# A pass of GpSimd before each scatter of the last two batch pairs, in place of waits on the shared expert, and two shared up products moved into the drain

## The reference, cut to what matters

```python
logits = x @ gate_weight.T                       # 4096 tokens, 64 experts
gidx = top_k(group_max(softmax(logits)), 3)      # 3 of 8 groups
topk_w, topk_i = top_k(masked_scores, 6)         # 6 experts for each token
pos = cumulative count of a token's expert, over all tokens in order
slot = flat * C + minimum(pos, C - 1)            # C = 96 rows for each expert
buf = zeros(E * C, H).at[slot].set(x[tok])
out = silu(buf @ Wg) * (buf @ Wu) @ Wd           # for each of 64 experts
y = sum over 6 of out[slot] * topk_w
shared = silu(x @ Sg.T) * (x @ Su.T) @ Sd.T      # for all tokens
result = x + layernorm(y + shared)
```

## Time and profile before

| what | value |
|---|---|
| median of three runs | 1271.32 us (1269.12 to 1275.74) |
| the profiled execution | 1273.42 us, of which its span is 1271.6 us |
| mean granted TensorE clock | 0.98 |
| PE busy | 1172.3 us (92%) |
| DVE busy | 943.0 us (74%) |
| ACT busy | 870.4 us (68%) |
| POOL busy | 658.9 us (52%), of which the 192 scatters to BUF take 201.3 us |

### The profile page before, as it was taken

How to read it: one execution, slowest core, us unless ns; L and a number is a source line. 1 busy time by engine, 2 the same in 40 slices (tenths; PEclk the granted TensorE clock), 3 DMA queues, 4 the chain that set the end, 5 groups by cost and what they waited for, 6 DMA issues and landing times.

```text
span 1271.6 us, 25022 instructions
## 1 busy us (share of the span) xinstructions
PE 1172.3 (92%) x7360; PEld 830.8 (65%) x7360; DVE 943.0 (74%) x2773; ACT 870.4 (68%) x2327; POOL 658.9 (52%) x742
## 2 busy tenths in 40 slices
PE   4899999999999999999999999999879798999984
PEld 1466766766676676676667667667635476878863
DVE  3897688789789889979988997988856245444536
ACT  3998779878877887887888788788624332333424
POOL 4564334336654655654565565566562624444556
PEclk9999999999999999999999999999988899999988
DMA  8686677867976765565566456456427389899676
GB/s 271 156 218 143 113 131 152 169 149 173 192 179 135 121 120 103 107 123 102 100 105 110 93 105 133 77 97 109 87 58 224 107 229 226 228 242 234 138 192 227
DMA packets 402184, 190.02 MB, mean 149 GB/s; under 512 B 319312, under 2 KB 386358, under 8 KB 402048
## 3 DMA queue, kind: packets, MB, share of 16 engines
q1 hardware_dynamic: 375968, 166.38, 58.3%
q0 software_dynamic: 16416, 11.70, 5.2%
q10 hardware_dynamic: 9664, 10.30, 2.8%
HBM read 75.32 MB, written 64.69 MB: 110 GB/s over the span
## 4 chain that ended last, share of the span: by engine, by line
PE 71%; DVE 10%; issue 6%; ACT 6%; DMA 6%; another core or an unknown queue 1%; SPq 1%; POOL 0%; ACTq 0%; DVEq 0%; POOLq 0%
PE bank L1151 15%; PE bank L1180 14%; PE bank L1195 11%; PE bank L1166 8%; PE bank L1212 8%; DMA Y<-W,wix 4%; PE bank L1336 3%; PE bank L1319 3%; PE bank L1244 3%; PE bank L1323 2%; PE bank L1278 1%; ACT P L1432 1%; DMA X<-in_x 1%; DVE nm L1627 1%; ACT unused L617 1%
## 5 line engine op out<-in xcount | busy, mean ns | idle before, releaser
L1432 ACT ACTIVATE P<-bank,nm 128x256 f32<-128x256 f32 x512 | 237.5, 470 | 106.4 <-DVE nm L1627 97.0
L1151 PE MATMUL bank<-RB,W 128*128 128x512 f16 x1076 | 276.7, 382 | 5.3 <-DVE W L820 3.9
L1180 PE MATMUL bank<-RB 128*128 128x256 f32 x1024 | 244.1, 381 | 10.1 <-issue 6.8
L1081 POOL TENSOR_SCALAR P<-P,rr 128x256 f32<-128x256 f32 x256 | 120.4, 478 | 251.9 <-DVE rr L1609 244.6
L831 POOL DMA_INDIRECT BUF<-RT,ix x192 | 201.3, 1048 | 78.7 <-issue 37.2
L1180 PEld LDWEIGHTS bank<-RB 128*128 128x128 f32 x1024 | 185.2, 191 | 34.6 <-ACT RB L1403 6.6
L1151 PEld LDWEIGHTS bank<-RB,W 128*128 128x128 f16 x1076 | 105.5, 99 | 124.4 <-issue 10.5
L1627 DVE TENSOR_REDUCE nm<-bank 128x2 f32<-128x512 f32 x256 | 174.0, 681 | 11.1 <-PE bank L1180 8.7
L1212 PE MATMUL bank<-W,O 128*128 128x256 f16 x1060 | 157.9, 274 | 6.8 <-issue 6.8
L1102 POOL DMA_INDIRECT Y<-W,wix x64 | 90.8, 1419 | 111.5 <-ACT W L1515 43.8
L1086 POOL TENSOR_TENSOR PH<-P,PH 128x512 f16<-128x512 f32 x86 | 101.3, 1178 | 87.9 <-ACT PH L1448 86.7
(11 more groups left out here) (251 smaller groups left out, 2032.5 us busy)
## 6 DMA issues: line engine op xcount, KB each, us to landing
RB<-in_ewT SPq DMA_DIRECT2D x24, 352.0 KB
BUF<-zrow SPq DMA_DIRECT2D x24, 321.0 KB, 3.3
W<-BUF ACTq DMA_DIRECT2D x58, 120.4 KB
HT<-in_ewT SPq DMA_DIRECT2D x18, 352.0 KB
HT<-in_wc SPq DMA_DIRECT2D x24, 256.0 KB, 4.4
HT<-in_ws SPq DMA_DIRECT2D x24, 256.0 KB, 5.1
Y<-zrow SPq DMA_DIRECT2D x20, 256.0 KB
X<-in_x SPq DMA_DIRECT2D x8, 512.0 KB, 4.5
```

The lines of the kernel that those rows point to most:

```text
L1081: r = eng.tensor_scalar(p, p, rr[:, w % 4, t:t + 1], SP_, ALU.mult, ALU.mult)
L1151: r = eng.matmul(bk_[:, :], W[:, m, a, c * 2048 + h * 128:c * 2048 + (h + 1) * 128], XT[:, bp % 2, b, c, :], start=(k == 0), stop=(k == n ...
L1180: r = eng.matmul(bS[u % 2][:, t * 256:(t + 1) * 256], QK[:, i % 2, 0, q * 256 + t * 128:q * 256 + (t + 1) * 128], QK[:, i % 2, 1, q * 256: ...
L1432: r = eng.activation(P[:, u % 2, t * 256:(t + 1) * 256], bS[u % 2][:, t * 256:(t + 1) * 256], ACT.Exp, bias=nm0[:, u % 4, t:t + 1], accum_ ...
```

## The change

Three things change. The table `REST` goes. Instead each of the 48 scatters of batch pairs 6 and 7 (`bp >= PAUSE_FROM`) is led by one GpSimd `tensor_scalar` over 128 x 256 zeros (`still`, float32) into scratch (`pause`, float16), which counts up a new semaphore, and the scatter waits until it has. And the up products U1 and U2 move from the head of the tail into the drain slots 257 and 259 of PE, with h0 and s1 in slot 257 of ACT and a1 in slot 258 of DVE.

```diff
-TAIL_ORDER = {'pe': 'U1 U2 U3 U4 D0 U5 ...
- 'dve': 'c6 l0 c7 a1 c10 a2 ...
- 'act': 'h0 s1 s2 h1 s3 ...
+TAIL_ORDER = {'pe': 'U3 U4 D0 U5 ...
+ 'dve': 'c6 l0 c7 c10 a2 ...
+ 'act': 's2 h1 s3 ...
-    ("pe", 257): [("PV", 4), ("WO", 7), ("WO", 6), ("bg", 0)],
+    ("pe", 257): [("PV", 4), ("WO", 7), ("WO", 6), ("U", 1), ("bg", 0)],
-    ("pe", 259): [("PV", 4), ("WO", 7), ("WO", 6), ("bg", 0)],
+    ("pe", 259): [("PV", 4), ("WO", 7), ("WO", 6), ("U", 2), ("bg", 0)],
-    ("act", 257): [("bg", 0), ("bg", 0), ("O", 5), ("hi_w", 3), ("bg", 0), ("bg", 0), ("bg", 0)],
+    ("act", 257): [("bg", 0), ("bg", 0), ("O", 5), ("hi_w", 3), ("h", 0), ("s", 1), ("bg", 0), ("bg", 0), ("bg", 0)],
-    ("dve", 258): [("bg", 0), ("O", 6), ("bg", 0), ("lo_w", 3), ("bg", 0), ("bg", 0), ("bg", 0)],
+    ("dve", 258): [("bg", 0), ("O", 6), ("bg", 0), ("lo_w", 3), ("bg", 0), ("bg", 0), ("a", 1), ("bg", 0)],
-REST = {(6, 11): 2, (6, 18): 5, (7, 3): 11, (7, 6): 12, (7, 9): 13, (7, 12): 14, (7, 15): 15, (7, 18): 16, (7, 21): 17}
+PAUSE_FROM = NP - 2
+        pause, pauses = unused[:, 0:D], [0]
+        still = zrow[:, 0:D]
-                        if (bp, t * 6 + k) in REST:
-                            eng.wait_ge(s["saf"], REST[bp, t * 6 + k])
+                        if bp >= PAUSE_FROM:
+                            eng.tensor_scalar(pause, still, 1.0, 0.0, ALU.mult, ALU.add).then_inc(s["pause"], 1)
+                            pauses[0] += 1
+                            eng.wait_ge(s["pause"], pauses[0])
                         eng.wait_ge(s["po"], n)
                         eng.wait_ge(s["bi"], 16 * NBZ)
                         eng.indirect_dma_start(BUF, ...)
```

More of the change, by code:

```diff
@@ L149, in places @@
     return at
-TAIL_ORDER = {'pe': 'U1 U2 U3 U4 D0 U5 U6 U7 c39 U8 c44 U9 D1 U10 c64 U11 D2 U12 U13 U14 c73 U15 D3 U16 U17 D4 D5',
- 'dve': 'c6 l0 c7 a1 c10 a2 c12 l1 c15 a3 c17 l2 c20 a4 c26 l3 c29 a5 c36 l4 l5 a6 a7 c43 l6 c47 l7 '
+TAIL_ORDER = {'pe': 'U3 U4 D0 U5 U6 U7 c39 U8 c44 U9 D1 U10 c64 U11 D2 U12 U13 U14 c73 U15 D3 U16 U17 D4 D5',
+ 'dve': 'c6 l0 c7 c10 a2 c12 l1 c15 a3 c17 l2 c20 a4 c26 l3 c29 a5 c36 l4 l5 a6 a7 c43 l6 c47 l7 '
        'a8 c59 a9 c68 l8 l9 c71 a10 l10 a11 c72 a12 l11 a13 c75 l12 l13 a14 a15 l14 l15 a16 a17 l16 '
        'l17',
- 'act': 'h0 s1 s2 h1 s3 h2 c19 s4 h3 h4 y0 s5 h5 s6 c37 s7 y1 c41 h6 h7 s8 c48 s9 h8 y2 s10 y3 h9 s11 '
+ 'act': 's2 h1 s3 h2 c19 s4 h3 h4 y0 s5 h5 s6 c37 s7 y1 c41 h6 h7 s8 c48 s9 h8 y2 s10 y3 h9 s11 '
        'h10 s12 y4 h11 h12 s13 s14 s15 h13 y5 h14 h15 s16 y6 y7 s17 h16 h17 y8 y9 y10 y11'}
@@ L376, in build @@
         lix = sb("lix", [64, 1], U32)
-        names = ("c0 cg cd gt S e r rs pn ph pld plp pv oh ol wo q ql k kl v vh vl xc po wm wh wl "
+        names = ("pause c0 cg cd gt S e r rs pn ph pld plp pv oh ol wo q ql k kl v vh vl xc po wm wh wl "
                  "lf lc tx th lt lh lp xr fo hd bi yi dd lb sw swh swl sg ssl saf sah sal sdn sy et ebt eg esl eac eo eow wix ec ez wt wtc wtl ids oth otl ep fv fq fa fp fd fs fn fb fx fy").split()
```

## The result

The changed kernel takes 1283.79 us in the median (1278.89 to 1287.56, four runs), the kernel before, run beside it, 1272.96 us (1269.12 to 1275.74, four runs): a ratio of 1.0083, 95% interval 1.0051 to 1.0115. It is slower, by some 10.5 us. The forecast was 1287.5 us with a range of 1278 to 1297. Two lines were added above the first functions concerned and two more in `scatter`, so line 817 of before is 819 of after, 831 is 835, 1304 is 1308, and so on.

A forecast was written before the change was run, and what follows sets the result against it. The last scatter, arriving together with PE's tail, was taken to release the expert stage; a period of 2.34 us against 1.27 gave +14.5, restart 1.6, together +16.1: 1289.5 us, less 2.1 for the median, 1287.4 (1287.5), range 1278 to 1297.

The forecast's parts named there:

- The own wait, 0.78: Paced scatters on GpSimd: from a pass's end to the start of the scatter waiting for it, 0.78 us each time.
- The pass, 0.48: Paced train on GpSimd: each TENSOR_SCALAR of 128 x 256 takes 0.48 us of the 2.34 us period.
- the scatter, 1.05: Paced train on GpSimd: each scatter takes 1.05 us, the mean of all 192, in the 2.34 us period.
- From the last scatter to the first turn, 4.5: End of the tail: PE's first expert-stage turn comes 4.5 us after the last scatter, through SyncE's row loads.
- the +14.5: Start of the expert stage: PE's first turn comes at 1037.2 us instead of 1022.66, +14.5 us.
- The restart, 1.6: PE's start of the expert stage after the longer wait, partly at the lower clock: 1.6 us charged, bounds 0 and 3.
- The move, hidden: U1 and U2 into the drain: PE's tail 5.5 us shorter, covered by later scatters; up to 4.5 us if uncovered.
- The standstills: Drain and tail: scatter trains suggested as cause of 27.6 us of unexplained idle pieces; removing them does not affect the total.
- A: Rival, scatter train: own wait nearly free, period 1.72 us, standstills go; -7.9 us, 1263.5 us; chance 0.09.
- B: Rival, scatter train: period in between, 2.0 to 2.1 us; within 0.5%, 1268 to 1275 us; chance 0.05.
- C: Rival, tail: passes, scatters and DVE lengthen each other; +7 us, 1294.5, or 1301.5 if every period; chance 0.12.
- D: Rival, tail: the pass does not part the trains, standstills stay; same time as the forecast, no separate chance.

The follow-up runs named there:

- Experiment 5: Changed kernel with passes of 128 x 10, each into its own scratch, and no scatter waiting for its pass: 1259.23 us, ratio 0.9897 to the kernel before.
- experiment 6: Changed kernel with all 48 full passes, each waiting for the pass before it instead of each scatter for its own: 1256.52 us, ratio 0.9831.
- experiment 3: Kernel before with `REST` replaced by the 48 passes and waits, U1 and U2 left at the head of the tail: 1284.62 us, ratio 1.0058.
- experiment 11: Kernel before, unchanged, profiled again on the third chip: 1251.96 us, ratio 0.9991 to the kernel before beside it.
- experiment 1: Kernel before with only U1, U2, h0, s1 and a1 moved into the drain, `REST` kept, no passes: 1276.85 us, ratio 1.0019.
- experiment 8: Changed kernel with pass and wait only ahead of every sixth scatter (8 of 48): 1262.66 us, ratio 0.9895.
- experiment 12: Changed kernel with a pass ahead of every third scatter, each waiting for the pass before it; second run, third chip: 1249.37 us, ratio 0.9976.
- experiment 7: Changed kernel with pass and wait only ahead of every third scatter (16 of 48): 1255.43 us, ratio 0.9845.
- experiment 9: Changed kernel with pass and wait ahead of every third scatter, U1 and U2 back at the tail's head; third chip: 1262.18 us, ratio 1.0070.
- experiment 2: Changed kernel without its passes and without `REST`, so nothing parts the scatters: 1291.93 us, ratio 1.0133.
- experiment 4: Changed kernel with passes of 128 x 10, each into its own scratch and each still waited for by its scatter: 1275.49 us, ratio 1.0001.

## Why the prediction was right

Sign, mechanism and range were right: a longer period of the scatters, paid in full because the last scatter releases the expert stage. The terms in turn.

*The own wait, 0.78.* Exact: 0.78 ahead of the paced scatters, taken from three waits for another engine. Experiment 5 shows what would have happened without it (0.17), and experiment 6 that the same 48 passes without it bring a gain, so that the loss hangs on it and not on the pass.

*The pass, 0.48 and the scatter, 1.05.* Measured 0.42 to 0.43 for most passes (mean 0.449) and 1.01 for most scatters (mean 1.043). The mean of 478 ns came from passes of attention with other operands. From the first paced scatter (919.88) to the last (1029.70), less 1.28 for the indirect DMA of line 878, 47 periods take 108.54 us, 2.31 each on the mean against 2.34: the last scatter ends at 1030.71, not at 1032.7, 2.0 us less.

*From the last scatter to the first turn, 4.5.* Too long: it is 3.28 (1030.71 to 1033.99), and 3.32 and 3.27 in the traces of experiments 5 and 3. PE's lateness is the smaller part of the 1.2 us: in the trace of before the rows of expert 0 have landed at 1022.29 and PE turns them at 1022.66. The larger part is the path itself, which took longer there. It is long too in two traces where the scatters run in trains and PE has been idle for over 4 us, 4.64 us in experiment 11 and 5.86 (1023.00 to 1028.86) in experiment 1:

```profile
1028.86 0.58 PE L1304 MATMUL bank<-ident,W 96*128 96x96 f32 x2 [4.48 <-DMA W<-BUF]
```

With passes, or with trains of three, it is 3.2 to 3.4 us in every trace; what lengthens it otherwise was not tested. The two errors together, 2.0 of the train and 1.2 of this leg, make the +11.3 us of the first turn out of the +14.5.

*The restart, 1.6.* Its sign is right, but the total does not show it. The clock did fall to 0.50 and was back at 1.00 some 7 us behind the first turn. The first five groups of matmuls in the chain behind it (L1323, L1327, L1323, L1327, L1340 of after) take 5.76 us, where the same five take 3.35 in the kernel before: 2.4 us more, inside the bounds of 0 and 3. But from the first turn to the end of the span the profiled execution of after took 243.1 us and that of before 248.9, with the longest wait ahead of it; over the traces of all the kernels this stretch takes 241 to 251 us, in no order that the wait explains (experiment 8, with PE busy up to the turn, 241.8; experiment 12, after 8 us of waiting, 250.6). What moves it stays open, and it is the reason why the profiled span of after is only 5.5 us longer where the medians differ by 10.8. It also means that a first turn tells the time of a kernel only to some 5 us.

*The move, hidden.* Right: experiment 3 loses it and differs from the full change by less than the intervals. Its value without cover was put at up to 4.5 us, and experiments 7 and 9 (on two chips) put it at 4.1 to 5.8. The prediction saw only the shorter tail of PE; the move also brings pair 7's indices some 6 us forward. That it could lengthen a train by releasing `REST` early, as in experiment 1, was not seen.

*The standstills.* That trains of scatters go with them was "suggested, not shown"; experiments 1 and 2 bear it out for the chips on which they occur, and experiment 11 shows a chip on which the same trains cause none. The forecast was independent of it, as stated, since the scatters set the end either way.

*The rivals.* A was the right picture of another kernel: at a period of 1.63 (experiment 6) its price of -7.9 us was too small. Its first turn came 14.7 us earlier than that of before, since pair 7's scatters began at 963.38 and not at 968.4 (A took 10 us off for the standstills and nothing for the move) and the last leg took 3.3 us and not 4.5. The measured gain is 20 us (1276.63 to 1256.52); where its rest arises is open, as the kernel before was not profiled on that chip. B's point of equality, 2.03, agrees with experiment 4 (2.06, no difference), though its first turn came 4.7 us later than in the trace of before, so luck has a part in it. C has its mechanism, at a small part of its price. By the Trainium skill's rule in SBUF — State Buffer, section Who interferes with whom, DVE instructions with two inputs in SBUF shut out the passes. The means (449 ns, 1043 ns) hide it, as they did in attention, where single passes of a mean of 478 ns take up to 984; single rows show it. In the kernel after, POOL and then DVE:

```profile
963.01 1.20 POOL L830 TENSOR_SCALAR unused<-zrow 128x256 f16<-128x256 f32 x1
...
988.79 0.61 POOL L830 TENSOR_SCALAR unused<-zrow 128x256 f16<-128x256 f32 x1
```

```profile
962.67 1.28 DVE L1662 TENSOR_TENSOR W<-W 96x512 f16<-96x512 f32 x2
...
988.46 1.48 DVE L1662 TENSOR_TENSOR W<-W 128x512 f16<-128x512 f32 x2
```

The first pass starts while two such DVE instructions run until 963.95, and ends 0.26 us behind them, after 1.20 in place of 0.42. By that rule, the trace agrees, and the prediction's reading of the mean was too coarse. Five of the 48 passes exceed the usual 0.42 us by 0.09 to 0.78, together 1.35 us, and each of the five overlaps a DVE instruction with two operands in SBUF. Eight of the 48 scatters exceed 1.01 us, together by 1.4. C had put 7 or 14 us on both. D is refuted: the passes do part the trains.

## What to carry to other kernels

When a wait is made to space out an engine's own work, look at whose completion it asks for: a wait for the instruction just before costs the engine its running ahead (0.78 against 0.17 us here, 48 times), the same wait one pass behind left 0.17 and no standstill. Before work is taken off one engine, find the other parents of the next stage and when each arrives: here PE was done 28 us earlier and the stage began 11 us later. And measure such a cure on more than one chip: on one where the kernel before has no standstills, the best version of these gains 0.2 to 0.4% and experiment 9 loses 0.7%; on the two others experiments 6 and 7 gain 1.6 to 1.7%.

## What the runs showed of the hardware that was not expected

- On two of three chips ACT, DVE and PE stopped together beside unbroken trains of GpSimd's indirect DMAs (one start each 1.27 us), for 20.6 us (21 in a train) and 27.6 us (27), with no releaser in the trace and a DMA share of 0.04. With a pass of 128x256 between two of them no standstill was left, with one of 128x10 and no wait one of 4.45 us; trains of three showed none, trains of six idle pieces of ACT and DVE of 4 to 8 us. On the third chip trains of 14 and of 25 stopped nothing. What the engines wait for was not found.
- A GpSimd instruction that waits for the GpSimd instruction just ahead of it starts 0.78 us after that one's end, as one that waited for VectorE did in three rows of before; one that need not wait starts after 0.17.
- A `tensor_scalar` of GpSimd takes 0.42 us over 256 columns and 0.22 over 10: 25 times the columns take not quite twice the time.
